# A macaron block (feed-forward, attention, feed-forward): the gate's product in column strips, and four moves of small work around it

## The reference

```python
x = x + 0.5 * ffn(layernorm(x))
x = x + attn(layernorm(x))                  # with weight and bias; causal; 8 heads of 8; unit q and k
x = x + 0.5 * ffn(layernorm(x))
...
def ffn(x):                                 # 8 experts, all evaluated for every token
    logits = x @ gate_w.T + gate_b
    ms = mean(logits * logits, axis=-1)
    logits = logits * rsqrt(ms + eps) * rms_w
    g = max(softmax(logits / 0.5))          # one weight per token
    norm_g = g / (g + 1e-6)
    h = gelu(einsum('nd,edh->neh', x, w1) + b1)
    y = einsum('neh,ehd->ned', h, w2) + b2
    return (y * norm_g[:, None, None]).sum(axis=1)
```

## Time and profile before

| | |
|---|---|
| median of 3 runs | 288.85 us (288.41 to 289.15) |
| the profiled execution | 288.67 us |
| its span, first to last instruction | 286.9 us |
| PE busy in the span | 274.2 us (96%) |
| DVE, ACT, POOL busy | 216.9, 222.8, 87.6 us |
| granted clock of PE, mean | 0.999 |

### The profile page before, as it was taken

The page is one execution under the profiler, slowest core; times in us unless marked ns, Lnnn a source line. Parts: engine busy times, 40 slices in busy tenths (PEclk is TensorE's granted clock), DMA queues, the critical chain, the costliest instruction groups (busy, mean ns, idle before and its releaser), DMA issues.

```text
span 286.9 us, 5191 instructions
## 1 busy us (share of the span) xinstructions
PE 274.2 (96%) x1651; PEld 191.6 (67%) x1651; DVE 216.9 (76%) x573; ACT 222.8 (78%) x346; POOL 87.6 (31%) x155
## 2 busy tenths in 40 slices
PE   8998999999989998899998999999999999999994
PEld 8675788788778886432433432378888888888882
DVE  7699989888989889855588153078788898797765
ACT  2766876868787785999999999976785877677672
POOL 6326203301890383361438321401300310310010
PEclk9999999999999999999999999999999999999999
DMA  5720000000000000000000000000001000100101
GB/s 156 233 73 1 0 1 2 0 0 1 2 1 0 3 1 0 0 2 2 0 3 0 3 0 2 0 2 0 0 2 39 0 0 0 37 0 2 38 0 37
DMA packets 8107, 4.64 MB, mean 16 GB/s; under 512 B 690, under 2 KB 8084, under 8 KB 8084
## 3 DMA queue, kind: packets, MB, share of 16 engines
q1 hardware_dynamic: 8084, 4.35, 5.3%
HBM read 3.30 MB, written 1.05 MB: 15 GB/s over the span
## 4 chain that ended last, share of the span: by engine, by line
PE 73%; POOL 8%; ACT 8%; issue 5%; DVE 4%; DVEq 0%; POOLq 0%; ACTq 0%
PE ps L494 9%; PE ps L489 9%; PE ps L471 8%; PE ps L477 8%; PE ps L474 8%; PE ps L492 8%; PE ps L625 8%; ACT probs L803 5%; PE ps L602 3%; PE ps L664 2%; PE ps L656 2%; PE ps L451 2%; PE ps L580 2%; PE ps L442 2%; POOL rstd L1231 1%
## 5 line engine op out<-in xcount | busy, mean ns | idle before, releaser
L790 ACT ACTIVATE h<-ps,cols 128x512 f32<-128x512 f32 x128 | 87.9, 691 | 48.8 <-PE ps L477 43.5
L958 DVE TENSOR_TENSOR h_lo<-h,h_hi 128x512 fp32r<-128x512 f32 x128 | 92.0, 724 | 29.6 <-ACT h_hi L793 27.1
L803 ACT ACTIVATE probs<-ps 128x1024 f32<-128x1024 f32 (+1 forms) x80 | 67.0, 1013 | 0.6 <-PE ps L602 0.4
L489 PE MATMUL ps<-h_hi,w_hi 128*128 128x512 f32 x128 | 52.9, 413 | 0.3 <-DVE h_hi L956 0.3
L494 PE MATMUL ps<-h_lo,w_hi 128*128 128x512 f32 x128 | 50.9, 398 | 1.4 <-DVE h_lo L958 1.4
L471 PE MATMUL ps<-xT_hi,w_hi 128*128 128x512 f32 (+1 forms) x128 | 50.7, 396 | 0.1
L477 PE MATMUL ps<-xT_lo,w_hi 128*128 128x512 f32 (+1 forms) x128 | 50.0, 391 | 0.0
L492 PE MATMUL ps<-h_hi,w_lo 128*128 128x512 f32 x128 | 50.0, 391 | 0.0
L474 PE MATMUL ps<-xT_hi,w_lo 128*128 128x512 f32 (+1 forms) x128 | 49.9, 389 | 0.0
L793 ACT ACTIVATE h_hi<-ps,cols 128x512 fp32r<-128x512 f32 x72 | 49.2, 683 | 0.0
L1312 POOL TENSOR_SCALAR_AFFINE_SELECT probs<-probs 128x256 f32<-128x256 f32 x64 | 26.0, 431 | 46.5 <-ACT probs L803 46.0
(11 more groups left out here) (130 smaller groups left out, 288.4 us busy)
## 6 DMA issues: line engine op xcount, KB each, us to landing
w_raw<-in_L_ffn_w SPq DMA_DIRECT2D x8, 256.0 KB, 4.9
x_sb<-in_L_attn_x SPq DMA_DIRECT2D x3, 256.0 KB, 6.8
out_x<-x_sb SPq DMA_DIRECT2D x3, 256.0 KB, 2.3
x_sb<-in_L_attn_x SPq DMA_DIRECT2D x2, 128.0 KB, 2.2
out_x<-x_sb SPq DMA_DIRECT2D x2, 128.0 KB, 1.8
wout_sb<-in_L_attn_w_out SPq DMA_DIRECT2D x8, 4.0 KB
wqkv_sb<-in_L_attn_w_qkv SPq DMA_DIRECT2D x1, 96.0 KB, 6.0
small<-in_L_ffn_b SPq DMA_DIRECT2D x1, 8.0 KB
```

Source lines behind the costliest of these rows:

```text
L489: pe.matmul(y, w2_hi[:, w], h_hi[:, c % RING, :], start=(c == 0), stop=False)
L790: first = nc.scalar.activation(h[:, slot, :], ps[:, BANK_H + slot, :], ACT.Gelu, bias=bias)
L803: nc.scalar.activation(probs[:, s % P_SLOTS, :, 0:width], ps[:, bank:bank + 2, 0:width], ACT.Exp, scale=SCALE).then_inc(exp_done, 1)
L958: dve.tensor_tensor(h_lo[:, slot, :], h[:, slot, :], h_hi[:, slot, :].bitcast(f32), ALU.subtract).then_inc(split_done, 1)
```

## The change

1. `gate_product` makes four products with the gate's 32 columns (8 weights, the rest without use) as stationary operand, one in each strip of 32 columns of PE, each with 32 tokens of every tile (128 moving columns). The result has experts on partitions; DVE transposes it in blocks of 32 into `gate_rows`, and then adds the bias. In the second layer's first group the product goes from c = 8 to c = 6.
2. POOL makes the low parts of the stacks ahead of the gate's root; the gate's shift, tanh and weight go one chunk later in the third and fourth group.
3. At the start the first two tiles have a root of their own, and DVE normalises them ahead of the low part of the first weights. The last quarter of w1 goes from c = 5 to c = 7, the gate's logits of the first group from c = 5 to c = 6.
4. The very last chunk's high part is made by ACT.

```diff
-AT_ZERO = dict(AT, ln_stats=(2, 3), ln_aggregate=4, gate_logits=5)
-AT_THIRD = dict(AT, ..., gate_shift=11, gate_tanh=12, gate_weight=13)
-AT_LAST = dict(AT, ..., gate_shift=11, gate_tanh=12, gate_weight=13, ...)
+AT_ZERO = dict(AT, ln_stats=(2, 3), ln_aggregate=4, gate_logits=6)
+AT_THIRD = dict(AT, ..., gate_shift=12, gate_tanh=13, gate_weight=14)
+AT_LAST = dict(AT, ..., gate_shift=12, gate_tanh=13, gate_weight=14, ...)
-AT_FIRST = dict(AT, gate_product=8, gate_logits=8, gate_shift=12, gate_tanh=13, gate_weight=14)
+AT_FIRST = dict(AT, gate_product=6, gate_logits=6, gate_shift=11, gate_tanh=12, gate_weight=13)
...
+        def vector_rounds(layer, c, F):
+            ends = isinstance(F, int) and F == 2 * GROUPS - 1 and c == CHUNKS - 1
+            return c in VECTOR_ROUNDS[layer] and not ends
...
-                for i in range(GROUP_TILES):
-                    m = pe.matmul(ps[:, BANK_GATE, EXPERTS * i:EXPERTS * i + EXPERTS], xf[:, FFN, P * i:P * i + P],
-                                  cols[:, COL_GATE:COL_GATE + EXPERTS], start=True, stop=True)
+                tokens = xf[:, FFN, :].rearrange("p (i s a) -> p s i a", i=GROUP_TILES, a=ROW)
+                for strip in range(P // ROW):
+                    m = pe.matmul(ps[ROW * strip:ROW * strip + ROW, BANK_GATE, 0:GROUP_TILES * ROW],
+                                  cols[:, COL_GATE:COL_GATE + ROW], tokens[:, strip, :, :], start=True, stop=True)
...
-                dve.tensor_tensor(logits[:, :, :], ps[:, BANK_GATE, 0:GROUP_TILES * EXPERTS].rearrange("p (t e) -> p t e", e=EXPERTS),
-                                  per_expert(gate_b_row[:, :]), ALU.add).then_inc(gate_logits_done, 1)
+                dve.transpose(gate_rows[:, :, :].rearrange("p t r -> p (t r)"),
+                              ps[:, BANK_GATE, 0:GROUP_TILES * ROW]).then_inc(gate_logits_done, 1)
                 dve.wait_ge(gate_logits_done, F + 1)
+                dve.tensor_tensor(logits[:, :, :], gate_rows[:, :, 0:EXPERTS], per_expert(gate_b_row[:, :]), ALU.add).then_inc(gate_self, 1)
...
-                    if layer == 0 and first and c in (0, 5):
-                        weight_parts(2 + c // 5)
+                    if layer == 0 and first and c in (0, 7):
+                        weight_parts(2 + c // 7)
...
             first_halves()
-            weight_parts(0)
-            normalise(FFN, 0, 0)
+            weight_high(0)
+            dve.wait_ge(rstd_first, 1)
+            for i in halves[0]:
+                dve.tensor_scalar(xn[:, FFN, i, :], x_tile(0, i), mean_var[:, FFN, i, 0:1], rstd[:, FFN, i:i + 1],
+                                  ALU.subtract, ALU.mult).then_inc(xn_done[FFN], 1)
+            weight_low(0)
+            normalise(FFN, 0, 0, halves[1])
...
+                if layer == 0 and g >= 2:
+                    low_parts(pool, g - 2)
                 gate_root(F)
                 if layer == 0 and g == 1:
                     ln_twice(g - 1)
-                if layer == 0 and g >= 2:
-                    low_parts(pool, g - 2)
...
-            ln_once(0)
+            pool.wait_ge(mv_done[FFN], 2)
+            pool.tensor_tensor(var_eps[:, FFN, 0:2], mean_var[:, FFN, 0:2, 1], ln_eps[:, 0:1].to_broadcast([P, 2]),
+                               ALU.add).then_inc(var_first, 1)
+            pool.wait_ge(var_first, 1)
+            pool.tensor_tensor(rstd[:, FFN, 0:2], var_eps[:, FFN, 0:2], neg_half[:, 0:1].to_broadcast([P, 2]),
+                               ALU.pow).then_inc(rstd_first, 1)
...
```

More of the change, by code:

```diff
@@ L131, in build @@
         b2_sb = sb("b2_sb", [EXPERTS, P])
-        cols = sb("cols", [P, SMALL + 1])
+        cols = sb("cols", [P, COL_GATE + ROW])
         gate_b_row = sb("gate_b_row", [P, EXPERTS])
@@ L148, in build @@
         xn = sb("xn", [P, 2, GROUP_TILES, DIM])
+        gate_rows = sb("gate_rows", [P, GROUP_TILES, ROW])
         logits = sb("logits", [P, GROUP_TILES, EXPERTS])
@@ L274, in v_of @@
             return v_ones[:, tiles, 4 * quad:4 * quad + 4, v_part(quad)]
-        def vector_rounds(layer, c):
-            return c in VECTOR_ROUNDS[layer]
+        def vector_rounds(layer, c, F):
+            ends = isinstance(F, int) and F == 2 * GROUPS - 1 and c == CHUNKS - 1
+            return c in VECTOR_ROUNDS[layer] and not ends
         def rounded_until(layer, F, c):
@@ L449, in gate_product @@
                 pe.wait_ge(gate_logits_done, F)
-                for i in range(GROUP_TILES):
-                    m = pe.matmul(ps[:, BANK_GATE, EXPERTS * i:EXPERTS * i + EXPERTS], xf[:, FFN, P * i:P * i + P],
-                                  cols[:, COL_GATE:COL_GATE + EXPERTS], start=True, stop=True)
+                if isinstance(F, int) and F == 0:
+                    pe.wait_ge(cols_zero, 1)
+                tokens = xf[:, FFN, :].rearrange("p (i s a) -> p s i a", i=GROUP_TILES, a=ROW)
+                for strip in range(P // ROW):
+                    m = pe.matmul(ps[ROW * strip:ROW * strip + ROW, BANK_GATE, 0:GROUP_TILES * ROW],
+                                  cols[:, COL_GATE:COL_GATE + ROW], tokens[:, strip, :, :], start=True, stop=True)
                 m.then_inc(gate_mm, 1)
@@ L482, in down @@
                 y = ps[:, BANK_Y, :]
-                if vector_rounds(layer, c):
+                if vector_rounds(layer, c, F):
                     pe.wait_ge(h_hi_done, rounded_until(layer, F, c))
@@ L790, in gelu @@
                 first = nc.scalar.activation(h[:, slot, :], ps[:, BANK_H + slot, :], ACT.Gelu, bias=bias)
-                if not vector_rounds(layer, c):
+                if not vector_rounds(layer, c, F):
                     nc.scalar.activation(h_hi[:, slot, :], ps[:, BANK_H + slot, :], ACT.Gelu, bias=bias).then_inc(gelu_done, 1)
@@ L1108, in first_halves, with weight_high @@
                     aggregate(FFN, halves[half])
-            def weight_parts(k):
+            def weight_high(k):
                 part = slice(PART * k, PART * k + PART)
@@ L1113, in weight_parts, with weight_low @@
                 dve.tensor_copy(w1_hi[:, part], w1_raw[:, part]).then_inc(w1_hi_ready, 1)
+            def weight_low(k):
+                part = slice(PART * k, PART * k + PART)
                 dve.wait_ge(w1_hi_ready, k + 1)
@@ L1116, in weight_parts @@
                                   ALU.subtract).then_inc(w1_ready, 1)
+            def weight_parts(k):
+                weight_high(k)
+                weight_low(k)
             def output(pair):
@@ L1291, in _ @@
             zero_fill(pool, slice(TILES // 2, TILES), const_self)
-            ln_once(0)
+            pool.wait_ge(mv_done[FFN], 2)
[4 more added lines that the diff above has]
+                               ALU.pow).then_inc(rstd_first, 1)
+            pool.wait_ge(mv_done[FFN], 4)
+            pool.tensor_tensor(var_eps[:, FFN, 2:4], mean_var[:, FFN, 2:4, 1], ln_eps[:, 0:1].to_broadcast([P, 2]),
+                               ALU.add).then_inc(var_done[FFN], 1)
+            pool.wait_ge(var_done[FFN], 1)
+            pool.tensor_tensor(rstd[:, FFN, 2:4], var_eps[:, FFN, 2:4], neg_half[:, 0:1].to_broadcast([P, 2]),
+                               ALU.pow).then_inc(rstd_done[FFN], 1)
             for k in range(4):
```

25 lines of the change are left out of this document (14 added, 11 removed).

## The result

The changed kernel takes 289.26 us in the median of 20 runs (288.79 to 290.09), the kernel before 288.78 (20 runs, 288.20 to 289.34): ratio 1.0021, 95% interval 1.0012 to 1.0030. The forecast was 288.5, a gain of 0.3; it became a loss of 0.5, a small one but beyond the measurement's uncertainty. The profiled execution took 289.08 us, 0.41 more than the one of before.

A forecast was written before the change was run, and what follows sets the result against it. PE bounds the second layer, while DVE leads in the first group. Terms 0 + 1.3 - 0.34 - 0.05 + 0 - 1.36 + 0.13 = -0.3 us on a median of 288.85 gave 288.5, range 287.2 to 289.7.

The forecast's parts named there:

- First group, +1.3: First layer, first group: DVE finishes normalising the tiles later, so PE's transposes come late; +1.3 us, upper bound 1.5.
- the first group loses nothing: Rival: DVE catches up before the tiles are needed, the 1.3 becomes about 0, time 287.2; chance 0.17.
- Gate in strips, 0.56: Each of eight gate products on PE: 0.56 us in four column strips instead of 0.90, saving 0.34.
- DVE's transpose, 0.22: Each gate adds one 128-column transpose out of PSUM on DVE, 0.22 us; slack for it outside the first group.
- Second and third group, -0.34 and -0.05: First layer: second group gains the gate's 0.34; in the third the stall moves from stacks to low features, -0.05.
- Fourth group, 0: First layer: stack transposes come 1.13 earlier, but the moved shift holds the tanh, so the first Exp stays; 0.
- Start, 0: Kernel start: the root in halves gains 0, since PE reaches these transposes only behind its warm-up matmuls; bounds 0 to -0.5.
- Second layer and last chunk: Second layer: four gates at full price, -1.36 us; last chunk rounded by ACT instead of DVE, +0.13.
- The failed step: Fourth group: tanh about 114.36 against 114.38, first Exp 1.63 later at 116.01 as before, PE's score products waiting for it.

The follow-up runs named there:

- the shift-alone kernel: The kernel before with only gate_shift, gate_tanh and gate_weight of the first layer's last group moved to c = 12, 13, 14: 289.26 us, ratio 1.0024.

## Why the prediction was wrong

- **First group, +1.3:** measured +1.30, through the chain on DVE that was named. But PE stops for another instruction: the upward product of chunk 12 for its weights, not the transposes for their tiles. Nor did PE wait "for exactly this" before: its wait of 1.01 was for chunk 9's low part at 27.51. The moved weights and logits alone cost 1.06, the strips with DVE's transpose alone 0.26 in this group. The rival "the first group loses nothing" is out.
- **Gate in strips, 0.56:** measured 0.56 to 0.57. The Trainium skill (TensorEngine Tiling (Array Packing), Key Properties) speaks of draining at a mode switch; the trace agrees on the way in, 0.09 (200.91 to 201.23 is 0.32, against 0.23 into the gate before). The prediction's similar amount on the way out isn't shown: the first plain product behind the strips takes 0.33 (201.59 to 201.92), and the one behind the old gate, without strips, took 0.32 (18.58 to 18.90).
- **DVE's transpose, 0.22:** 0.34 from its start to the next instruction's (26.67 to 27.01), it lasts 0.31. No wait outside the first group was traced to it.
- **Second and third group, -0.34 and -0.05:** -0.31 and -0.05. **Fourth group, 0:** the stacks gain 1.08 (forecast 1.13), the tanh loses 1.10. That the 1.13 came out is luck: the forecast gave all of it to the root's order and left this group's gate out. The order is worth 0.70 in this group (24.50 against 25.20 with it undone) and the strips alone 0.38 (25.20 against 25.58); together they make the 1.08. The shift undone is worth 1.0 to 1.3 in the medians.
- **Start, 0:** undoing the halves changes nothing that shows. The +0.22 between the two profiled executions lies within the scatter of the start: over 18 profiled kernels with one of two programs at the start the first upward product lies between 8.10 and 8.80. What decides it stays open.
- **Up to the first Exp** the sum was +0.91 and the measurement is +0.96. **Second layer and last chunk**, -1.36 + 0.13 = -1.23: measured -1.18, of which the last chunk is +0.11 (3.54 against 3.43).
- **The failed step** is the one in the fourth group's term, "the table load and the first Exp come behind the tanh, 1.63 later at 116.01, as before", with nothing counted behind it: the sum passes from the first Exp to the second layer at no cost. There the attention takes +0.40 in the profiled execution: the late Exp itself makes it 0.18 shorter (69.72 in every execution with the late Exp and no fall, 69.90 to 69.92 with the early one where no wait is filled), and the fall of PE's granted clock to 0.50 makes it 0.58 longer, with ACT waiting for scores. Where the first group's stall is filled, about 0.9 separates the runs with and without a fall. That PE's idle time is needed for it is shown by the filled waits: with three of them filled, no fall in 21 runs of three kernels, and the attention 0.58 shorter in the changed one. Idle time alone isn't enough: the shift-alone kernel has the same waits without a fall. The second place is the first group, behind the stall that the forecast itself had found: a fall there costs 1.1 more by the profiles, and 5 of the 20 runs after, with a granted clock of 0.982, take 289.8 to 290.1. In profiles it is seen in three of the six kernels that have this stall unfilled, and in none of the others.
- **In numbers:** the profiled pair differs by +0.41 where -0.3 was forecast: 0.40 from the attention, 0.22 from the start, 0.05 each from the stages up to the first Exp and from the second layer. Without the fall the changed kernel would be 0.40 ahead of the kernel before at the last transposes, counted from the first upward product, about what was forecast. The medians, +0.48, can't be taken apart in this way: half of the runs before look like they have a fall of their own, and no run's start is known but the profiled ones'.

Not settled: why the fall comes in every run after, in about half of those before, in 3 of the 12 with the shift alone and in 10 of the 12 with the shift undone. Neither how much PE idles nor how the idle time is spread over these slices tells it: before and after have 2.61 of 4.00 us busy between 118 and 122, and the two executions with 1.34 and then 1.28 or 1.27 differ in their clock. Nor is it shown why the 0.37 in the second group goes with the weights' place.

## What to carry to other kernels

Where an instruction is moved out of a wait, ask first what the wait then holds: the weights' quarter cost nothing because DVE was waiting for POOL's root anyway, and 2.3 us in the medians, falls of the clock included, once it stood behind. Cost a new stall of TensorE twice, as a wait and as a fall of its granted clock that can come behind it, and look at the windows' clock column and at each run's mean clock, not at the median alone. A change whose parts nearly cancel is worth taking apart: strips and root order together with the old places of weights and shift, and later logits, gave 284.94 where the whole gave 289.26.

## What was not expected of the hardware

- The granted clock falls in the middle of a kernel whose PE is busy for 95% of the span: behind a slice with PE busy for 1.00 of 2.00 us in the attention, and in some executions behind the first group's stall (no matmul started from 26.81 to 28.94). The Trainium skill, TensorE: Matmul & The Clock Gate, Part 1, says that the clock has two levels, set by how busy the engine has been. The traces agree on the levels, since no slice is below 0.50 and several stand at it, and on the cause as far as filled waits end the falls; two executions with the same waits, one with and one without a fall, show that the busy time of these slices alone doesn't decide.
- What a fall costs differs: between executions with and without one it is 0.5 to 1.3 us in an attention that ACT leads (eight profiled executions), and 1.1 in the first group. In the changed kernel's profile the three low slices take 1.72 us of full clock away ((0.20 + 0.50 + 0.16) x 2 us), and the attention gets 0.58 longer.
- Useless matmuls in PE's waits save time in one kernel (287.75 against 289.26) and, at the same places of the attention, cost 0.65 us in the attention of another, where PE had no wait at one of them and another engine's wait grew.
